# State space kernel of the first block: gains on VectorE in fewer operations, column factors and one group's masks on GpSimd, fillers on TensorE

## The chip, the cores and the metric

One core of a Trainium2 chip runs the whole program in one launch. The metric is the device time of one execution in microseconds (us). Five engines work beside each other, each through its own list of instructions in order: TensorE (PE; its weight loads are shown as PEld), VectorE (DVE), ScalarE (ACT), GpSimd (POOL) and SyncE (SP, which only issues DMAs here). They wait for each other through semaphores. The execution that was profiled has its own time and its own span (first to last instruction); the sums below are made against that one.

## The reference, cut to what matters

Eight layers follow each other on x of 2 x 512 x 128 floats: attention and feed-forward blocks of several kinds. The change touches the first layer alone. There, per batch of 512 tokens:

```
scores = q k / sqrt(32) over 77 context rows, 4 heads;  attn = softmax of the 32 largest, 0 elsewhere
c_t    = (mean of attn over the heads) @ V                       # film input
x      = layernorm(x) * (1 + gate * scale_in(c_t)) + gate * shift_in(c_t)
dt = exp(log_dt);  dtA = dt * (A_re + i A_im);  dC = (C_re + i C_im) * (exp(dtA) - 1) / A
K[d, l] = 2 * Re sum_n dC[d, n] * exp(dtA[d, n] * l)             # 128 channels, 64 states, l < 512
y = causal convolution of x with K (by DFT), + x * D_skip
y = y * (1 + gate * scale_out(c_t)) + gate * shift_out(c_t);  x_text + y, feed-forward, layernorm
```

All values are float32.

## The kernel before, in words

Tokens are 8 tiles of 128 (tile t: 4 tiles to a batch). Two strands run side by side in this layer and meet in the DFT on TensorE.

**The scores strand.** ScalarE copies the scores s0 of each tile out of PSUM. VectorE takes the tiles in four groups of two (`vec_top`, L422): four rounds of eight MAX8 (L429) and eight MATCH_REPLACE8 (L440) strike the 32 largest of each row out of r0; after the first round L437 makes nb0 (the maximum, negated). ScalarE makes exp into e0 (`act_exps0`, L455) and the sums over the 32 (`act_sums0`, L462). VectorE then zeroes what was not struck (`vec_mask0`, L443: one operation a tile, r0 < limit times e0, L447) and makes the weights w0 (`vec_weight0`, L449, L452 and L453). ScalarE writes diagonals of w0 (`act_diag`, L479), TensorE sums the heads (L509), ScalarE copies (L489), TensorE makes the film (L516), ScalarE and VectorE (`vec_film`, L745 and L748) read it; the result xk goes to the DFT.

**The state space strand.** l is split in 32 x 16, so K is a matrix product of 128 partitions (64 states, real and imaginary part) between a column factor hh4 (32 values of l a channel) and a row factor gg4 (16 values). GpSimd makes the angles and multiplies them out (`pool_s4`, L644 and L647). VectorE takes off whole turns (`vec_phase`, L558: a tensor_scalar L560 and a scalar_tensor_tensor L561 over 2176 or 2048 elements a partition, in `vec_s4` for three tensors: columns, cosines gg4, sines sG). ScalarE makes sines (`act_s4_columns`, `act_s4_turns`) and decays (eH, eG at L688). VectorE multiplies hh4 by eH in eight operations of 512 (L577). GpSimd computes the gains al and be of each state from 24 operations of 128 (`pool_s4_gains`, L600 to L623) and then, in four quarters of the channels, the row factor (`pool_s4_rows`, L658 to L661: gg4 * al + sG * be, times eG). As each quarter arrives, TensorE multiplies 32 channels (`pe_kernel`, L706, 64 records of 16 columns in the trace) and ScalarE copies (`act_kernel`, L718).

Each engine's order is written out by hand (TensorE L2708, ScalarE L2759, GpSimd L2822, VectorE L2881). On TensorE it is: three kernel quarters, film of group 0, the last quarter, film of group 1, the DFT of K (L772), the DFT of batch 0 (L758), film of group 2, and so on. SP's load of the DFT matrices waits until VectorE has read the angles that lie in the same memory (L357). GpSimd has after the rows: x2 (`pool_x2`, the normalised x times g plus b, L736 and L737), `pool_add_row` (L257, b_out onto X), the skip terms (`pool_skip`, L836 to L839). `st.link` makes the engine wait for the instruction just issued. `pe_spin` (L267) issues matmuls whose result nobody reads.

Of the kernel before, what the change touches and what calls it, by code (L numbers as in the profile page):

```python
# [83 lines left out]
def program(nc, A, out):  # L84

    ctx = ExitStack()
    with ctx:
# [240 lines left out]
        gg4, sG, eG = (part(arenaB, 8416 + 2048 * i, D, LB) for i in range(3))  # L328
        V_H, V_GC, V_GS, V_HH = 3, 4, 5, 6
        s4_vec, s4_pe, s4_inverses = sem("s4_vec"), sem("s4_pe"), sem("s4_inverses")  # L330

# [90 lines left out]
        def vec_top(dve, st, g, rounds):  # L422
            if rounds[0] == 0:
                dve.wait_ge(s0_copy, 2 * g + 2)
            for k in rounds:
                src = s0 if k == 0 else r0
                for t in GROUPS[g]:
                    for h in range(H0):
                        ins = nc.vector.max(top0[:, t, h, 8 * k:8 * k + 8], src[:, t, h, :])  # L429
                if k < KEEP // 8 - 1:  # L430
                    st.link(ins)
                else:
                    ins.then_inc(top_ready, 1)
# [7 lines left out]
                st.link(ins)  # L441

        def vec_mask0(dve, g):  # L443

            for t in GROUPS[g]:
                dve.wait_ge(e0_ready, t + 1)
                nc.vector.scalar_tensor_tensor(e0[:, t], r0[:, t], 0.5 * NEVER, e0[:, t], ALU.is_lt, ALU.mult).then_inc(em_ready, 1)  # L447
# [102 lines left out]

        A_ARE, A_ANG, A_VH, A_UG, A_GAIN = 2, 3, 4, 5, 6
        E_TANH, E_ANG, E_H, E_X2, E_COLS, E_GC, E_GS, E_ROWS = 1, 2, 3, 4, 6, 7, 8, 9
# [19 lines left out]
        def vec_s4_columns(dve):  # L572

            dve.wait_ge(s4_act, E_COLS)
            for d in range(0, D, D // 8):
                r = slice(d, d + D // 8)
                ins = nc.vector.tensor_tensor(hh4[:, r], hh4[:, r], eH[:, r], ALU.mult)  # L577
            ins.then_inc(s4_vec, 1)

        em1, half_sin, full_sin, u0, inv_a2, u1, u2, u3 = (q[i][:] for i in (0, 1, 2, 3, 4, 5, 6, 7))  # L580

        def vec_s4_inverses(dve, st):
# [9 lines left out]
            L(Vv.reciprocal(u1, u2))  # L592
            Vv.tensor_tensor(u1, u1, em1, ALU.mult).then_inc(s4_inverses, 1)

        def pool_s4_gains(pool, st):
            L = st.link
            tt, ts = nc.gpsimd.tensor_tensor, nc.gpsimd.tensor_scalar
            pool.wait_ge(s4_inverses, 1)
            pool.wait_ge(s4_act, E_ANG)
            ts(em1, u1, 2.0, None, ALU.mult)  # L600
            L(tt(u0, half_sin, half_sin, ALU.mult))
            L(ts(u0, u0, 2.0, None, ALU.mult))
            tt(u2, em1, full_sin, ALU.mult)
            L(tt(u1, em1, u0, ALU.mult))
            tt(u2, u2, full_sin, ALU.add)
            L(tt(u1, em1, u1, ALU.subtract))
            L(tt(u1, u1, u0, ALU.subtract))
            tt(u0, u1, V["are"], ALU.mult)
            L(tt(u3, u2, V["aim"], ALU.mult))
            tt(u2, u2, V["are"], ALU.mult)  # L610
            L(tt(u0, u0, u3, ALU.add))
            tt(u0, u0, inv_a2, ALU.mult)
            L(tt(u3, u1, V["aim"], ALU.mult))
            L(tt(u2, u2, u3, ALU.subtract))
            L(tt(u2, u2, inv_a2, ALU.mult))
            tt(u1, V["cre"], u0, ALU.mult)
            L(tt(u3, V["cim"], u2, ALU.mult))
            L(tt(u1, u1, u3, ALU.subtract))
            ts(al[:], u1, 2.0, V["sgn"], ALU.mult, ALU.mult)
            tt(u2, V["cre"], u2, ALU.mult)  # L620
            L(tt(u3, V["cim"], u0, ALU.mult))
            L(tt(u1, u2, u3, ALU.add))
            ts(be[:], u1, -2.0, None, ALU.mult).then_inc(s4_pool, 1)  # L623
            pool.wait_ge(s4_pool, A_GAIN)

# [26 lines left out]
        def pool_s4_rows(pool, st, slices):  # L652
            L, tt = st.link, nc.gpsimd.tensor_tensor
            pool.wait_ge(s4_act, E_ROWS)
            for i in slices:
                r = slice(i * D // 4, (i + 1) * D // 4)
                gq, sq, n = gg4[:, r, :], sG[:, r, :], D // 4
                tt(gq, gq, bc(al[:, r], P, n, LB), ALU.mult)  # L658
                L(tt(sq, sq, bc(be[:, r], P, n, LB), ALU.mult))
                L(tt(gq, gq, sq, ALU.add))  # L660
                tt(gq, gq, eG[:, r, :], ALU.mult).then_inc(s4_pool, 1)  # L661
# [29 lines left out]
        def act_s4_turns(act):  # L691
            A_ = nc.scalar.activation
            act.wait_ge(s4_vec, V_GC)
            A_(gg4[:], gg4[:], ACT.Sin, scale=-TURN, bias=V["qturn"]).then_inc(s4_act, 1)
            act.wait_ge(s4_vec, V_GS)
            A_(sG, sG, ACT.Sin, scale=-TURN, bias=V["oturn"]).then_inc(s4_act, 1)

        def pe_kernel(pe, i):

            pe.wait_ge(s4_vec, V_HH)  # L700
            pe.wait_ge(s4_pool, A_GAIN + 1 + i)
            if i >= 2:
# [2006 lines left out]
        def _(pe):  # L2709
# [50 lines left out]
        def _(act):  # L2760
# [62 lines left out]
        def _(pool):  # L2823
# [58 lines left out]
        def _(dve):  # L2882
# [63 lines left out]
def _packed(I):  # L2946
# [9 lines left out]
    def chunks(a):  # L2956
# [89 lines left out]
```

## Time and profile before

| | us |
|---|---|
| three runs | 521.46, 520.95, 516.23; median 520.95 |
| profiled execution, its time | 518.91 |
| its span | 517.1 |
| busy in the span: PE, DVE, ACT, POOL | 448.2, 363.3, 280.2, 214.3 |

In the rows below, a time of the timeline is "start, length, engine, line, operation, out<-in, count"; in brackets stands what ended the idle time before. An operation that is held up by another engine's hold on memory shows as a longer operation, not as idle time. [...]

### The profile page before, as it was taken

How to read it: one execution, taken by the hardware profiler on the slowest of the kernel's cores; microseconds unless marked ns; L12 is line 12 of the kernel's file. 1: busy time of each engine (PE TensorE's matmuls, PEld its weight loads, DVE VectorE, ACT ScalarE, POOL GpSimd, SP SyncE). 2: the span in 40 equal slices, each digit the busy share in tenths (PEclk: the TensorE clock that was granted, in tenths of full speed). 3: DMA queues.
4: the chain of work that ended last, by engine and by line, in shares of the span. 5: the costliest groups of instructions: out<-in, count | busy, mean ns of one | idle time of the engine just before them, and what ended most of it. 6: DMA issues, size and time to landing. Idle time of an engine off the chain costs nothing.

```text
span 517.1 us, 9756 instructions
## 1 busy us (share of the span) xinstructions
PE 448.2 (87%) x3171; PEld 330.7 (64%) x3171; DVE 363.3 (70%) x1329; ACT 280.2 (54%) x891; POOL 214.3 (41%) x242
## 2 busy tenths in 40 slices
PE   3970489999888999998878998999899999699986
PEld 2320489889663467677745654677569997378855
DVE  4799988956568377685379585887673245889675
ACT  2698477641422566663334553666425567779543
POOL 4999996031114540000040155312447758423341
PEclk9665559999999999999997999999999999899999
DMA  7207000000419000000000141000346981100001
GB/s 253 96 1 308 12 1 3 2 1 1 162 40 419 18 2 1 1 2 2 1 0 12 38 114 35 1 2 1 99 129 196 298 271 55 41 0 2 1 0 43
DMA packets 20536, 34.45 MB, mean 67 GB/s; under 512 B 2627, under 2 KB 14083, under 8 KB 19942
## 3 DMA queue, kind: packets, MB, share of 16 engines
q1 hardware_dynamic: 19014, 30.80, 17.8%
q0 software_dynamic: 1472, 3.03, 1.6%
q8 instruction: 26, 0.43, 0.3%
q14 instruction: 24, 0.20, 0.1%
HBM read 29.00 MB, written 6.81 MB: 69 GB/s over the span
## 4 chain that ended last, share of the span: by engine, by line
PE 60%; DVE 14%; POOL 11%; DMA 5%; ACT 4%; issue 3%; SPq 1%; ACTq 0%; DVEq 0%; POOLq 0%
PE bank L270 3%; PE bank L1055 3%; PE bank L2385 3%; PE bank L792 3%; PE bank L1101 3%; PE bank L1082 3%; PE bank L2351 3%; PE bank L1998 2%; PE bank L706 2%; PE bank L1725 2%; DVE arenaB L440 2%; PE bank L1698 2%; PE bank L2375 2%; PE bank L263 2%; PE bank L874 1%
## 5 line engine op out<-in xcount | busy, mean ns | idle before, releaser
L270 PE MATMUL bank<-in_ctx 128*128 128x512 f32 (+2 forms) x130 | 43.5, 464 | 0.0
L219 POOL TENSOR_SCALAR rtmp<-mv 128x4 f32<-128x4 f32 x12 | 3.0, 253 | 95.6 <-DVE mv L198 77.0
L2096 POOL DMA_INDIRECT ys_scratch<-arenaB,home x30 | 28.9, 964 | 10.7 <-ACT arenaB L2055 7.1
L2430 ACT ACTIVATE arenaB<-bank,arenaB 128x77 f32<-128x77 f32 x88 | 27.2, 355 | 7.4 <-DVE arenaB L2471 7.4
L270 PEld LDWEIGHTS bank<-in_ctx 128*128 128x128 f32 x130 | 21.4, 198 | 14.8 <-issue 13.9
L2240 DVE TENSOR_TENSOR in_ffn<-in_dft,bank 128x256 f32<-128x256 f32 x30 | 12.4, 420 | 25.6 <-PE bank L2016 17.7
L1112 DVE TENSOR_REDUCE nmax<-bank 128x1 f32<-128x512 f32 x32 | 20.5, 685 | 13.2 <-PE bank L1055 13.2
L440 DVE MATCH_REPLACE8 arenaB<-arenaB 128x77 f32<-128x77 f32 x128 | 26.8, 223 | 0.0
L1165 ACT ACTIVATE arenaB<-bank,nmax 128x512 f32<-128x512 f32 x32 | 21.7, 683 | 4.3 <-DVE nmax L1112 2.6
L2343 POOL TENSOR_TENSOR arenaB<-arenaB 128x385 f32<-128x385 f32 x8 | 13.4, 1679 | 19.8 <-DVE arenaB L2333 19.8
L277 ACT COPY xnT<-bank 128x512 f32<-128x512 f32 x14 | 8.4, 597 | 24.4 <-PE bank L263 24.4
L226 POOL TENSOR_SCALAR rtmp<-mv 128x4 f32<-128x4 f32 x10 | 2.5, 248 | 45.8 <-DVE mv L198 39.6
L2065 ACT ACTIVATE in_dft<-bank 128x256 f32<-128x256 f32 x30 | 11.5, 383 | 17.8 <-PE bank L1998 17.8
L2089 POOL DMA_INDIRECT xs_scratch<-arenaB,slot x16 | 15.7, 981 | 12.4 <-issue 12.4
L2430 ACT ACTIVATION_READ_ACCUMULATOR arenaB<-bank,arenaB 128x1 f32 x88 | 20.8, 237 | 0.0
L2351 PE MATMUL bank<-arenaB,xnT 128*128 128x385 f32 (+1 forms) x48 | 20.1, 556 | 0.0
L1998 PE MATMUL bank<-in_dft 128*128 128x128 f32 x144 | 19.1, 276 | 1.0 <-DMA in_dft<-in_moe_dram 1.0
L429 DVE MAX8 arenaB<-arenaB 128x8 f32<-128x77 f32 x128 | 19.5, 225 | 0.3
L2385 PEld LDWEIGHTS bank<-arenaB 128*128 128x128 f32 (+1 forms) x160 | 18.6, 192 | 1.0 <-issue 0.7
L2385 PE MATMUL bank<-arenaB 128*128 128x128 f32 (+1 forms) x160 | 19.0, 275 | 0.0
L263 PE MATMUL bank<-in_ctx,xn 128*128 128x128 f32 x56 | 13.2, 335 | 6.4 <-DVE xn L233 6.1
L233 DVE TENSOR_SCALAR xn<-X,mv,rstd 128x128 f32<-128x128 f32 x56 | 16.0, 349 | 3.7 <-POOL rstd L220 2.8
(511 smaller groups left out, 1375.7 us busy)
## 6 DMA issues: line engine op xcount, KB each, us to landing
in_dft<-in_moe_dram SPq DMA_DIRECT2D x18, 256.0 KB
arenaA<-in_moe_dram SPq DMA_DIRECT2D x1, 3840.0 KB
tmp<-in_moe_dram SPq DMA_DIRECT2D x12, 256.0 KB
in_dft<-in_dft_dram SPq DMA_DIRECT2D x1, 2048.0 KB, 7.7
in_dft<-in_head_dram SPq DMA_DIRECT2D x1, 2048.0 KB, 7.6
arenaA<-in_l_dram SPq DMA_DIRECT2D x1, 2048.0 KB
xs_scratch<-in_spare_dram SPq DMA_DIRECT2D x2, 975.0 KB
arenaB<-xs_scratch SPq DMA_DIRECT2D x6, 260.0 KB, 4.8
```

The lines of the kernel that those rows point to most:

```text
L233: nc.vector.tensor_scalar(dst[:, t, :], src[:, t, :], mv[:, t, 0:1], rstd[:, t:t + 1], ALU.subtract, ALU.mult).then_inc(ln_done, 1)
L263: ins = nc.tensor.transpose(bank[banks[t // TB]][:, (t % TB) * P:(t % TB + 1) * P], src[:, t, :], ident)
L270: nc.tensor.matmul(bank[into][:, 0:width], ident, packed["ctx"][:, 0:width], start=True, stop=True)
L429: ins = nc.vector.max(top0[:, t, h, 8 * k:8 * k + 8], src[:, t, h, :])
L440: ins = nc.vector.match_replace(r0[:, t, h, :], top0[:, t, h, 8 * k:8 * k + 8], src[:, t, h, :], NEVER)
L1112: Vv.tensor_reduce(nmax0[:, t, h:h + 1], bank[2 * (n % 2) + i][:], AX.X, ALU.max, negate=True).then_inc(sc_max, 1)
L1165: nc.scalar.activation(pb0[:, n % 2, i, :], bank[2 * (n % 2) + i][:], ACT.Exp, bias=nmax0[:, t, h:h + 1], accum_out=rsum0[:, t, h:h + 1]). ...
L1998: ins = nc.tensor.matmul(bank[i % 4][:, c * P:(c + 1) * P], wtile[i % AHEAD][:, c * P:(c + 1) * P], xsT[:, g % 2, (i - i0) * P:(i - i0 + 1 ...
L2096: nc.gpsimd.indirect_dma_start(out=A[f"ys_scratch{b}"], out_offset=bass.IndirectOffsetOnAxis(ap=home[:, b, j:j + 1], axis=0), in_=ys[b][:, ...
L2351: nc.tensor.matmul(bank3(n, i)[:, 0:(h1 - h0) * NC], xnT[:, n * P:(n + 1) * P], f3[:, n // TB, h0:h1, :].rearrange("p h k -> p (h k)"), st ...
L2385: ins = nc.tensor.matmul(bank[6 + t % 2][:, 0:P], pT3[0:w, t % 2, c, :], vw3[0:w, t // TB, c, :], start=(c == 0), stop=(c == CK3 - 1))
L2430: ins = nc.scalar.activation(p3[:, n % 3, h, :], bank3(n, i)[:, (h - h0) * NC:(h - h0 + 1) * NC], ACT.Exp, bias=mx3[:, n % 3, h:h + 1], ac ...
```

## The change

- The sine of the row factor is no longer made from phases of its own: the cosine's phase is the sine's absolute value shifted. `vec_s4` takes the first phase with offset 0, and one scalar_tensor_tensor (max of the value and its negative) replaces the second `vec_phase`. Both turns on ScalarE then wait for V_GS.
- The 24 operations of `pool_s4_gains` become 18 on VectorE (`vec_s4_gains`), which stand after `vec_s4`, in front of group 1 of the scores.
- The eight column multiplications go to GpSimd (`pool_s4_columns`), after `pool_gate`, `pool_add_row` and both `pool_x2`, which now stand ahead of the rows; the rows wait for VectorE's gains.
- The masks of group 2 go to GpSimd (`pool_mask0`, four operations of 308, after the rows); VectorE's mask of group 3 waits for them, and group 3's first round of `vec_top` is moved ahead of the weights of group 2.
- ScalarE's copies for a later layer's folded weights are split around the decays of the rows, exponentials of group 1 move ahead of the first kernel quarter.
- TensorE gets fillers of 512 columns: four after the folds, one after each of the first two kernel quarters.

```diff
-            vec_phase(st, gg4, gg4, uG, V["quarter"]).then_inc(s4_vec, 1)
-            vec_phase(st, sG, sG, uG, V["off2"]).then_inc(s4_vec, 1)
-            dve.wait_ge(s4_vec, V_GS)
+            vec_phase(st, gg4, gg4, uG, 0.0).then_inc(s4_vec, 1)
+            dve.wait_ge(s4_vec, V_GC)
+            nc.vector.scalar_tensor_tensor(sG, gg4, -1.0, gg4, ALU.mult, ALU.max).then_inc(s4_vec, 1)
...
+        def vec_s4_gains(dve, st):
+            dve.wait_ge(s4_act, E_ANG)
+            stt(u0, half_sin, 2.0, half_sin, ALU.mult, ALU.mult)
+            L(stt(u2, em1, 1.0, full_sin, ALU.add, ALU.mult))
+            tt(al[:], u2, V["aim"], ALU.mult)
+            L(stt(u3, em1, 1.0, u0, ALU.add, ALU.mult))
...
+            stt(be[:], em1, V["sgn"], half_sin, ALU.mult, ALU.add).then_inc(s4_vec, 1)
...
+        def pool_mask0(pool, st):
+            pool.wait_ge(em_ready, 4)
+            pool.wait_ge(top_final, 1)
+            for t in GROUPS[2]:
+                st.link(nc.gpsimd.tensor_scalar(r0[:, t], r0[:, t], 0.5 * NEVER, None, ALU.is_lt))
+                pool.wait_ge(e0_ready, t + 1)
+                nc.gpsimd.tensor_tensor(e0[:, t], r0[:, t], e0[:, t], ALU.mult).then_inc(em_ready, 1)
...
         def pool_s4_rows(pool, st, slices):
-            pool.wait_ge(s4_act, E_ROWS)
+            pool.wait_ge(s4_vec, V_GAIN)
+            pool.wait_ge(s4_act, E_GS)
...
 # TensorE
             pe_fold1(pe)
+            pe_spin(0, 4, S)
             pe_kernel(pe, 0)
+            pe_spin(0, 1, S)
             pe_kernel(pe, 1)
+            pe_spin(0, 1, S)
...
 # GpSimd
-            pool_s4_gains(pool, st)
             pool_gate(pool)
-            pool_s4_rows(pool, st, range(4))
+            pool_add_row(pool, V["b_out"], NT)
             pool_x2(pool, st, 0)
             pool_x2(pool, st, 1)
-            pool_add_row(pool, V["b_out"], NT)
+            pool_s4_columns(pool)
+            pool_s4_rows(pool, st, range(4))
+            pool_mask0(pool, st)
...
 # VectorE
             vec_s4(dve, st)
-            vec_s4_columns(dve)
+            vec_s4_gains(dve, st)
             vec_top(dve, st, 1, range(4))
...
-            vec_top(dve, st, 2, range(2, 3))
+            vec_top(dve, st, 2, range(2, 4))
             vec_film(dve, st, 1)
-            vec_top(dve, st, 2, range(3, 4))
-            vec_mask0(dve, 2)
+            vec_top(dve, st, 3, range(1))
             vec_weight0(dve, st, 2)
-            vec_top(dve, st, 3, range(4))
+            vec_top(dve, st, 3, range(1, 4))
             vec_mask0(dve, 3)
```

## Rows read from the trace of the kernel before

**Rows 1.** Windows by stage: second half of the first layer's DFT.
```profile
104.00:135.00 31.00, 30.78 (x241) 28.31 (x242) 15.79 (x46) 6.54 (x27) 6.33 (x6) 1.00 0.00 1
```

**Rows 2.** Chain that ended last, in order of time (start, length, engine, line).
```profile
29.44 0.50 POOL xt L600
...
54.04 1.02 POOL arenaB L658
...
63.73 3.57 PE bank L706 x64
```

**Rows 3.** Timeline of VectorE: phases, columns, start of group 1.
```profile
30.68 1.39 DVE L560 TENSOR_SCALAR arenaB<-arenaA,in_cols 128x2176 f32<-128x2176 f32 x1
32.11 2.55 DVE L561 SCALAR_TENSOR_TENSOR arenaA<-arenaB,arenaA 128x2176 f32<-128x2176 f32 x1
...
38.44 1.48 DVE L560 TENSOR_SCALAR arenaB<-in_dft,in_cols 128x2048 f32<-128x2048 f32 x1
...
42.41 6.87 DVE L577 TENSOR_TENSOR arenaA<-arenaA 128x512 f32<-128x512 f32 x8
49.20 1.21 DVE L429 MAX8 arenaB<-arenaB 128x8 f32<-128x77 f32 x8
```

**Rows 4.** Timeline of GpSimd: a gain, row angles, x2, b_out, skip.
```profile
25.21 4.24 POOL L647 TENSOR_TENSOR in_dft<-tmp,in_cols 128x512 f32<-128x512 f32 x4
...
32.34 2.63 POOL L604 TENSOR_TENSOR xt<-xt 128x128 f32<-128x128 f32 x1
...
76.33 1.27 POOL L736 TENSOR_TENSOR tmp<-tmp,in_rows 128x512 f32<-128x512 f32 x1
...
78.90 2.36 POOL L257 TENSOR_TENSOR X<-X,in_rows 128x1024 f32<-128x1024 f32 x1
...
86.93 1.26 POOL L838 TENSOR_TENSOR tmp<-tmp,xnT 128x512 f32<-128x512 f32 x1
88.27 1.39 POOL L839 TENSOR_TENSOR tmp<-tmp,xn 128x512 f32<-128x512 f32 x1
```

**Rows 5.** Timeline of VectorE: masks and small operations beside GpSimd, last mask alone.
```profile
66.03 1.20 DVE L437 TENSOR_SCALAR nb<-arenaB 128x8 f32<-128x8 f32 x1
...
74.05 1.00 DVE L453 TENSOR_TENSOR w<-w,tmask 128x8 f32<-128x8 f32 x1
...
86.99 3.01 DVE L447 SCALAR_TENSOR_TENSOR arenaB<-arenaB 128x308 f32<-128x308 f32 x2
...
102.48 0.87 DVE L447 SCALAR_TENSOR_TENSOR arenaB<-arenaB 128x308 f32<-128x308 f32 x2
```

**Rows 6.** Timeline of VectorE: operations of 128; the first is waited for.
```profile
12.58 0.28 DVE L587 TENSOR_TENSOR xt<-in_s 128x128 f32<-128x128 f32 x1
12.90 0.29 DVE L588 TENSOR_TENSOR xt<-xt 128x128 f32<-128x128 f32 x1
```

**Rows 7.** Timelines of ScalarE and TensorE: column sine, row decays, diagonals, last quarter, DFT.
```profile
37.02 2.10 ACT L683 ACTIVATE arenaA<-arenaA,in_cols 128x2048 f32<-128x2048 f32 x1
...
45.73 3.75 ACT L688 ACTIVATE arenaB<-tmp 128x128 f32<-128x128 f32 x16
...
77.79 2.45 ACT L479 ACTIVATE diag<-in_ctx,w 128x128 f32<-128x128 f32 x8
...
77.36 2.20 PE L706 MATMUL bank<-arenaB,arenaA 128*32 128x16 f32 x64
...
83.44 7.31 PE L772 MATMUL bank<-kx,in_dft 128*128 128x128 f32 x64
...
104.22 3.81 PE L758 MATMUL bank<-arenaA,in_dft 128*128 128x128 f32 x32 [0.85 <-DVE arenaA L748]
```

**Rows 8.** Page: largest group of TensorE (the filler's line), and load of DFT matrices.
```profile
L270 PE MATMUL bank<-in_ctx 128*128 128x512 f32 (+2 forms) x130 | 43.5, 464 | 0.0
...
in_dft<-in_dft_dram SPq DMA_DIRECT2D x1, 2048.0 KB, 7.7
```

**Rows 9.** Windows of two us: score matmuls at half clock.
```profile
32.00:34.00 2.00, 2.00 (x4) 0.65 (x3) 1.97 (x2) 1.98 (x8) 2.00 (x2) 0.50 0.00 0
```

More of the change, by code:

```diff
@@ L328, in program @@
         gg4, sG, eG = (part(arenaB, 8416 + 2048 * i, D, LB) for i in range(3))
-        V_H, V_GC, V_GS, V_HH = 3, 4, 5, 6
-        s4_vec, s4_pe, s4_inverses = sem("s4_vec"), sem("s4_pe"), sem("s4_inverses")
+        V_H, V_GC, V_GS, V_GAIN, V_HH = 3, 4, 5, 6, 7
+        s4_vec, s4_pe, top_final = sem("s4_vec"), sem("s4_pe"), sem("top_final")
         def quarters():
@@ L440, in vec_top @@
                         ins = nc.vector.match_replace(r0[:, t, h, :], top0[:, t, h, 8 * k:8 * k + 8], src[:, t, h, :], NEVER)
-                st.link(ins)
+                if g == 2 and k == KEEP // 8 - 1:
+                    ins.then_inc(top_final, 1)
+                else:
+                    st.link(ins)
+        def pool_mask0(pool, st):
[5 more added lines that the diff above has]
+                nc.gpsimd.tensor_tensor(e0[:, t], r0[:, t], e0[:, t], ALU.mult).then_inc(em_ready, 1)
         def vec_mask0(dve, g):
+            if g == 3:
+                dve.wait_ge(em_ready, 6)
             for t in GROUPS[g]:
@@ L549, in pe_dt @@
             nc.tensor.matmul(bank[7][:, 0:D], V["avg"], dtd, start=True, stop=True).then_inc(s4_pe, 1)
-        A_ARE, A_ANG, A_VH, A_UG, A_GAIN = 2, 3, 4, 5, 6
+        A_ARE, A_ANG, A_VH, A_UG, A_HH = 2, 3, 4, 5, 6
         E_TANH, E_ANG, E_H, E_X2, E_COLS, E_GC, E_GS, E_ROWS = 1, 2, 3, 4, 6, 7, 8, 9
@@ L567, in vec_s4, with pool_s4_columns @@
             dve.wait_ge(s4_vec, V_H)
-            vec_phase(st, gg4, gg4, uG, V["quarter"]).then_inc(s4_vec, 1)
-            vec_phase(st, sG, sG, uG, V["off2"]).then_inc(s4_vec, 1)
-            dve.wait_ge(s4_vec, V_GS)
-        def vec_s4_columns(dve):
-            dve.wait_ge(s4_act, E_COLS)
+            vec_phase(st, gg4, gg4, uG, 0.0).then_inc(s4_vec, 1)
+            dve.wait_ge(s4_vec, V_GC)
+            nc.vector.scalar_tensor_tensor(sG, gg4, -1.0, gg4, ALU.mult, ALU.max).then_inc(s4_vec, 1)
+        def pool_s4_columns(pool):
+            pool.wait_ge(s4_act, E_COLS)
             for d in range(0, D, D // 8):
                 r = slice(d, d + D // 8)
-                ins = nc.vector.tensor_tensor(hh4[:, r], hh4[:, r], eH[:, r], ALU.mult)
-            ins.then_inc(s4_vec, 1)
+                ins = nc.gpsimd.tensor_tensor(hh4[:, r], hh4[:, r], eH[:, r], ALU.mult)
+            ins.then_inc(s4_pool, 1)
         em1, half_sin, full_sin, u0, inv_a2, u1, u2, u3 = (q[i][:] for i in (0, 1, 2, 3, 4, 5, 6, 7))
@@ L592, in vec_s4_inverses @@
             L(Vv.reciprocal(u1, u2))
-            Vv.tensor_tensor(u1, u1, em1, ALU.mult).then_inc(s4_inverses, 1)
-        def pool_s4_gains(pool, st):
+            Vv.scalar_tensor_tensor(em1, u1, 2.0, em1, ALU.mult, ALU.mult)
+        def vec_s4_gains(dve, st):
             L = st.link
[L597 to L607, printed above, removed]
+            tt, stt = nc.vector.tensor_tensor, nc.vector.scalar_tensor_tensor
+            dve.wait_ge(s4_act, E_ANG)
[3 more added lines that the diff above has]
+            L(stt(u3, em1, 1.0, u0, ALU.add, ALU.mult))
+            tt(be[:], u2, V["are"], ALU.mult)
+            L(tt(u1, em1, u3, ALU.subtract))
@@ L608, in pool_s4_gains @@
             tt(u0, u1, V["are"], ALU.mult)
[L609 to L612, printed above, removed]
             L(tt(u3, u1, V["aim"], ALU.mult))
-            L(tt(u2, u2, u3, ALU.subtract))
-            L(tt(u2, u2, inv_a2, ALU.mult))
+            tt(u0, u0, al[:], ALU.add)
+            L(tt(u2, be[:], u3, ALU.subtract))
+            stt(u0, u0, 2.0, inv_a2, ALU.mult, ALU.mult)
@@ L616, in pool_s4_gains @@
+            L(stt(u2, u2, 2.0, inv_a2, ALU.mult, ALU.mult))
             tt(u1, V["cre"], u0, ALU.mult)
[L617 to L624, printed above, removed]
+            tt(u3, V["cim"], u2, ALU.mult)
@@ L628, in pool_s4 @@
+            tt(em1, V["cre"], u2, ALU.mult)
+            L(tt(half_sin, V["cim"], u0, ALU.mult))
+            stt(al[:], u1, V["sgn"], u3, ALU.mult, ALU.subtract)
+            stt(be[:], em1, V["sgn"], half_sin, ALU.mult, ALU.add).then_inc(s4_vec, 1)
         def pool_s4(pool, st):
@@ L657, in pool_s4_rows @@
                 gq, sq, n = gg4[:, r, :], sG[:, r, :], D // 4
-                tt(gq, gq, bc(al[:, r], P, n, LB), ALU.mult)
-                L(tt(sq, sq, bc(be[:, r], P, n, LB), ALU.mult))
-                L(tt(gq, gq, sq, ALU.add))
+                tt(gq, gq, bc(be[:, r], P, n, LB), ALU.mult)
+                L(tt(sq, sq, bc(al[:, r], P, n, LB), ALU.mult))
+                L(tt(gq, sq, gq, ALU.subtract))
+                if i == slices[0]:
+                    pool.wait_ge(s4_act, E_ROWS)
                 tt(gq, gq, eG[:, r, :], ALU.mult).then_inc(s4_pool, 1)
@@ L692, in act_s4_turns @@
             A_ = nc.scalar.activation
-            act.wait_ge(s4_vec, V_GC)
-            A_(gg4[:], gg4[:], ACT.Sin, scale=-TURN, bias=V["qturn"]).then_inc(s4_act, 1)
             act.wait_ge(s4_vec, V_GS)
+            A_(gg4[:], gg4[:], ACT.Sin, scale=-TURN).then_inc(s4_act, 1)
             A_(sG, sG, ACT.Sin, scale=-TURN, bias=V["oturn"]).then_inc(s4_act, 1)
         def pe_kernel(pe, i):
-            pe.wait_ge(s4_vec, V_HH)
-            pe.wait_ge(s4_pool, A_GAIN + 1 + i)
+            pe.wait_ge(s4_pool, A_HH + 1 + i)
             if i >= 2:
@@ L1215, in act_fold1, with act_fold1_out @@
             nc.scalar.copy(bm1[:], bank[3][0:DC, 0:D]).then_inc(fold1_copy, 1)
+        def act_fold1_out(act):
             act.wait_ge(fold1_mm, 3)
@@ L2773, in _ @@
             act_s4_turns(act)
+            act_fold1(act)
             act_s4_rows(act)
+            act_fold1_out(act)
             act_exps0(act, 0)
@@ L2777, in _ @@
             act_vfilm(act)
-            act_fold1(act)
+            act_exps0(act, 1)
             act_kernel(act, 0)
-            act_exps0(act, 1)
+            act_sums0(act, 1)
             act_kernel(act, 1)
-            act_sums0(act, 1)
             act_diag(act, 0)
@@ L2978, in _packed @@
         "alt": np.tile([1.0, -1.0], (P, 1)), "quarter": np.repeat([0.25, 0.0], P // 2)[:, None],
-        "off2": np.repeat([0.0, 0.25], P // 2)[:, None], "qturn": TURN * np.repeat([0.25, 0.0], P // 2)[:, None], "oturn": TURN * np.repeat([0.0, 0.25], P // 2)[:, None],
+        "off2": np.repeat([0.0, 0.25], P // 2)[:, None], "qturn": TURN * np.repeat([0.25, 0.0], P // 2)[:, None], "oturn": np.full((P, 1), 0.25 * TURN),
         "sgn": np.repeat([1.0, -1.0], P // 2)[:, None],
```

2 lines of the change are left out of this document (1 added, 1 removed).

## The prediction

> **What bounds the kernel now.** I read the windows first, then the chain of waits, then each engine's timeline where the chain changes engine. In the windows TensorE is busy for 30.78 of the 31 us from 104 to 135 [rows 1]: whatever is worth having in this layer lies ahead of that. The chain of waits names the owner: GpSimd from 29.44 (the gains) through 54.04 (the first row operation) to TensorE's second kernel quarter at 63.73 [rows 2]; and at 104.22 begins the DFT's second batch, for which TensorE waited 0.85 us on VectorE [rows 7]. From that instant TensorE decides, so a delay of it at about 83 or 104 reaches the end of the span in full, and an early arrival is worth as much as VectorE is early too.
>
> The timelines tell why 24 operations of 128 on GpSimd took 24 us. One of them lasted 2.63 us from 32.34 on [rows 4]; that is VectorE's scalar_tensor_tensor of 2.55 us from 32.11 on [rows 3]. It goes the other way as well: two masks on VectorE took 3.01 us beside GpSimd's skip operations of 1.26 and 1.39 us and 0.87 us alone, and an operation on eight numbers took 1.20 us [rows 4, 5]. Laid on one time line, VectorE's first mask (86.99) begins to work when L838 ends (88.2), L839 then waits for it, and the second mask ends (90.0) after L839 (89.66). So the two engines take turns, one whole instruction each, whenever both read this memory with two inputs or VectorE runs a tensor_scalar; MAX8 and MATCH_REPLACE8 are not held. The eight columns bear it out: 6.87 us, 0.86 each, one small GpSimd operation to each of them [rows 3].
>
> **The change, part by part.** I take four holds from these rows: a GpSimd operation of 512 holds 1.1 us (1.06 back to back at L647, 1.27 whole at L736 [rows 4]); a VectorE tensor_scalar of 2048 or 2176 holds 1.2 (1.39 less the end of a small GpSimd operation), a scalar_tensor_tensor of that size 2.3 (2.55 likewise), an operation of 128 holds 0.2 of its 0.28 [rows 3, 6].
>
> *Phases.* One tensor_scalar (1.48 [rows 3]) goes. Five long operations stay, with other company. GpSimd is free at 29.44, does the gate (256 wide, under the 1.27 us of an operation of 512, and VectorE is in MATCH_REPLACE8) and begins to add b_out by 30.4 to 30.7, with VectorE's phase due at 30.68; were the phase first, the order of the turns changes and their sum does not. That addition is 2.36 us long [rows 4], so the phase starts at 32.8. From there they take turns: VectorE 34.0, x2 35.1, VectorE 37.4, x2 38.5, VectorE 39.7, x2 40.8, VectorE 43.0, x2 44.1, absolute value 46.4. Before, this stretch ended at 42.41 [rows 3]. So 1.5 us saved and 5.5 lost: +4.0.
>
> *Columns and gains.* The columns' sines are ready by then (they need only the first phase, at 37.4, and two sines of ScalarE of 2.1 us [rows 7]), so GpSimd's eight operations of 512 meet VectorE's 18 gains. Eight turns of 1.1 + 0.2 take 10.4 us: 56.8. Ten gains are left, alone: 0.28 each, 2.8 us (0.32 where the next waits for it [rows 6]). VectorE is through at 59.6, and GpSimd's rows, which wait for it, begin at 59.6 where they began at 54.04: +5.6. By the row, eight columns take 6.87 us on VectorE and at least 8.5 on GpSimd; I cost them by their own rows, 1.1 each.
> [...]
>
> *ScalarE.* Both turns now follow the absolute value; then the folds' copies and the row decays (3.75 us [rows 7]). They end near 56, needed only at the last operation of the first quarter, after 62. Nothing. If the gains were 6 us earlier than I say, they would bind.
>
> *Scores on VectorE.* Group 1 starts at 59.6 instead of 49.20 [rows 3]: +10.4. From there to the weights of group 1 (74.05 + 1.00 [rows 5]) was 25.85 us, of which some 5 were turns given to GpSimd's rows. The rows last four quarters of 4.85 (54.04 to 63.73 is two) and end at 79.0, so the second pair of masks and weights is no longer held: 1.8 us less. Weights of group 1: 59.6 + 24.05 = 83.65. ScalarE began the diagonals from them at 77.79 [rows 7], then idle capacity of 2.7 us; now it begins at 83.65, +5.9. From the diagonals to the DFT of K there were 5.65 us (77.79 to 83.44 [rows 7]), and the last kernel quarter (rows at 79.0, matmuls after film 0) is done by 83. The DFT starts at 89.3.
>
> *Masks of group 2.* 3.01 us leave VectorE [rows 5]. Four GpSimd operations of 308, each under the 2.36 us of one of 1024, start when the last round of group 2 is struck (about 91) and end before 100; the film of group 2 needs them at 105, VectorE's mask 3 at 105. Behind them waits only the skip of batch 0, needed at the first result, after 120. Nothing, with 5 us of cover.
>
> *End of the layer.* VectorE's chain, three us lighter and delayed by 8.6 at 83.65, reaches film 2 at 105; TensorE reaches it 5.9 late. So of the 0.85 us that TensorE waited at 104.22 some 0.5 go. Sum: +5.9 - 0.5 = **+5.4 us**.
>
> *Fillers and DMA.* Six fillers of 0.46 us at mostly full clock [rows 8] lie in TensorE's waits for the rows: a quarter of 3.57 us plus one filler, 4.0 to 4.5, fits the 4.85 between quarters. The DFT load goes out 4 us later (46.4), takes 7.7 [rows 8] and is needed at 89. Both nothing.
>
> The profiled execution took 518.91 us (517.1 of span). 518.91 + 5.4 = **524.3 us**. The median shown is 2.0 above the profiled time, so by it the same step would read 526.4.
>
> **Bounds.** Twelve GpSimd operations of 512 at 1.06 instead of 1.1 give 0.5 back, at 1.27 cost 2.0 more; turns that VectorE wins now and then give up to 2 back. Alone, my case is 522 to 527.
>
> **Rivals.**
>
> *A, forecast: the two engines take turns and the rows start late.* 524.3. Chance 0.45.
>
> *B, half of it: the long phases are held, but VectorE's short gains slip through beside the columns.* For it: no row shows two-input operations of 128 on VectorE against operations of 512 on GpSimd for long. Then the gains end near 51, the columns at 55, rows +1.0, group 1 +1.8, both inside the slack of 2.7 us. If the fillers also bring TensorE to the full clock one quarter earlier, a quarter costs 2.20 instead of 3.57 us [rows 2, 7]. Together +1 to -2: 517 to 520. Chance 0.18.
>
> *C, other side: faster.* Mechanism: GpSimd's operations don't delay VectorE here, only their own completion. Place: 30.7 to 46. The phases end at 41, the gains at 45.5, group 1 starts 3.7 us earlier; with the masks gone VectorE reaches film 2 about 6.7 earlier. GpSimd: 32.8, x2 37.9, columns from 41 to 48, rows 6 us earlier. Price -6.3: 512.6. It decides as soon as rows start before 54.04 and group 1 before 49.20. Against it stand three rows [rows 5]. Chance 0.22.
>
> *D: A, and TensorE meets the DFT at half clock.* In A TensorE waits between the films, from 75 to 89, where it ran through before. The DFT of K at half clock would take up to twice 7.31 us [rows 7]; half of that at half clock is +3.7: 528. The rows are of two minds: at 32 to 34 TensorE was busy all the time and the granted clock was 0.50 [rows 9].
> [...] Chance 0.15.
>
> **How the numbers follow.** What a measurement of this kernel can tell from no change is about 1%, 5.2 us. A lies just at it: half of its chance is within. Faster: C but for a little, 0.21. Within 1%: B and half of A, 0.41. Slower: half of A and D, 0.38. A and D hold 0.6, B and C 0.4, so the range has to take in C: 512 to 530; the likeliest case's own is 522 to 527.
>
> **What would show it.** In the changed kernel: VectorE's first phase longer than 3 us, since it begins under the b_out addition (C: 1.4); the column operations on GpSimd spaced by 1.3 us with a gain between each two (B and C: 1.06); the first row operation at 59 to 60 (C: 48); group 1's first MAX8 at 59 to 60 (C: 45); the DFT of K starting at 89 (C: 77); the granted clock at that start (D: 0.50). If the rows begin before 54, or the b_out addition doesn't push the phase, the prediction is wrong.

## The result, and the profile after

| | before | after |
|---|---|---|
| median of four runs each, us | 520.44 | 525.29 |
| profiled execution, us | 518.91 | 524.83 |
| its span, us | 517.1 | 523.0 |

The ratio of the medians is 1.0105, with a 95% interval of 1.0066 to 1.0145: the change makes the kernel slower by about 1%, 4.85 us by the medians. 524.3 us had been forecast, 5.4 us above the profiled execution of the kernel before.

VectorE's timeline of the changed kernel (start, length, engine, line, operation, operands, count) answers to [rows 3] and [rows 6]:

```profile
31.26 3.14 DVE L573 TENSOR_SCALAR arenaB<-arenaA,in_cols 128x2176 f32<-128x2176 f32 x1
...
43.31 3.23 DVE L583 SCALAR_TENSOR_TENSOR arenaB<-arenaB 128x2048 f32<-128x2048 f32 x1
46.47 1.36 DVE L612 SCALAR_TENSOR_TENSOR xt<-xt 128x128 f32<-128x128 f32 x1
...
55.41 1.35 DVE L619 TENSOR_TENSOR xt<-xt,in_s 128x128 f32<-128x128 f32 x1
56.80 0.29 DVE L620 TENSOR_TENSOR xt<-xt,tmp 128x128 f32<-128x128 f32 x1
...
59.06 0.35 DVE L629 SCALAR_TENSOR_TENSOR tmp<-xt,in_cols 128x128 f32<-128x128 f32 x1
59.32 1.21 DVE L429 MAX8 arenaB<-arenaB 128x8 f32<-128x77 f32 x8
...
83.40 0.17 DVE L466 TENSOR_TENSOR w<-w,tmask 128x8 f32<-128x8 f32 x1
```

And GpSimd's, which answers to [rows 4]:

```profile
30.90 2.35 POOL L257 TENSOR_TENSOR X<-X,in_rows 128x1024 f32<-128x1024 f32 x1
...
35.59 3.33 POOL L741 TENSOR_TENSOR tmp<-tmp,in_rows 128x512 f32<-128x512 f32 x1
...
44.37 12.25 POOL L590 TENSOR_TENSOR arenaA<-arenaA 128x512 f32<-128x512 f32 x8
59.48 1.06 POOL L662 TENSOR_TENSOR arenaB<-arenaB,tmp 128x512 f32<-128x512 f32 x1 [2.87 <-DVE tmp L629]
...
77.69 1.26 POOL L667 TENSOR_TENSOR arenaB<-arenaB 128x512 f32<-128x512 f32 x1
90.62 0.99 POOL L450 TENSOR_SCALAR arenaB<-arenaB 128x308 f32<-128x308 f32 x1 [11.67 <-DVE arenaB L440]
```

Read the two side by side. The first phase, 1.39 us before, takes 3.14 beside the b_out addition; GpSimd's x2 products, of which one took 1.27 us before [rows 4], take up to 3.33 beside VectorE's long operations, and its eight column products 12.25 beside the last phase and the gains. Eight gains take 1.24 to 1.36 us each while GpSimd does its eight columns, and the ninth, L620 at 56.80, takes 0.29 again. The rows wait 2.87 us for the last gain.

TensorE's timeline answers to [rows 7]:

```profile
64.30 2.20 PE L710 MATMUL bank<-arenaB,arenaA 128*32 128x16 f32 x64 [2.35 <-POOL arenaB L667]
...
74.06 3.60 PE L710 MATMUL bank<-arenaB,arenaA 128*32 128x16 f32 x64 [0.55 <-POOL arenaB L667]
77.58 3.58 PE L522 MATMUL bank<-diag,arenaB 128*77 128x128 f32 x16
...
82.83 2.20 PE L710 MATMUL bank<-arenaB,arenaA 128*32 128x16 f32 x64
84.98 2.24 PE L522 MATMUL bank<-diag,arenaB 128*77 128x128 f32 x16
...
89.26 7.31 PE L776 MATMUL bank<-kx,in_dft 128*128 128x128 f32 x64
...
109.55 3.81 PE L762 MATMUL bank<-arenaA,in_dft 128*128 128x128 f32 x32 [0.36 <-DVE arenaA L752]
```

The DFT of K begins at 89.26 (83.44 before), the second batch's products at 109.55 (104.22): +5.33 of the span's +5.9. From 74.06 to the end of L522 at 87.2 TensorE has no idle time, and in the middle it runs at half the clock. The windows (from:to, length, PE busy and count, granted TensorE clock as a share of full speed, DMA share, GB/s; in [rows 1] and [rows 9] the busy times and counts of PE, PEld, DVE, ACT and POOL stand between length and clock) show where:

```profile
68.00:70.00 2.00, 0.98 (x31) 1.00 0.00 0
70.00:72.00 2.00, 2.00 (x40) 0.67 0.00 0
...
80.00:82.00 2.00, 2.00 (x12) 0.77 0.00 0
82.00:84.00 2.00, 2.00 (x42) 1.00 0.00 0
```

The start of the first phase differs from profile to profile (30.68 us in the kernel before, 30.85 to 32.52 in the twelve others, among which no edit stands ahead of it). So kernels are compared below by instants counted from that start ("from the phase").

| from the phase, us | rows start | third quarter starts | group 1's weights done | DFT of K | second batch |
|---|---|---|---|---|---|
| before | 23.33 | 37.96 | 44.37 | 52.76 | 73.54 |
| changed | 28.22 | 42.80 | 52.31 | 58.00 | 78.29 |

From the second batch's products to the end of the span the thirteen profiles, these two and the eleven of the runs, have 411.0 to 413.7 us left, in no order that goes with an edit; those differences I leave unexplained.

### The profile page after: what moved, and what is told of

Same layout as the page of the kernel before. It is cut to its first block, busy times and chain, and to the rows that moved or that the text cites. A ratio compares the mean times of both kernels' runs of the same rounds, so it can differ in the third digit from the quotient of the medians.

```text
span 523.0 us, 9775 instructions
## 1 busy us (share of the span) xinstructions
PE 453.5 (87%) x3183; PEld 330.6 (63%) x3183; DVE 368.8 (71%) x1336; ACT 279.8 (53%) x891; POOL 213.2 (41%) x230
## 4 chain that ended last, share of the span: by engine, by line
PE 63%; DVE 18%; POOL 5%; DMA 5%; ACT 4%; issue 3%; SPq 1%; ACTq 0%; DVEq 0%; POOLq 0%
PE bank L270 3%; PE bank L1059 3%; PE bank L2390 3%; PE bank L796 3%; PE bank L1105 3%; PE bank L762 3%; PE bank L1086 3%; PE bank L2356 2%; PE bank L2003 2%; PE bank L1730 2%; PE bank L1703 2%; PE bank L263 2%; PE bank L2380 2%; PE bank L878 1%; PE bank L522 1%
## 5 line engine op out<-in xcount | busy, mean ns | idle before, releaser
L270 PE MATMUL bank<-in_ctx 128*128 128x512 f32 (+2 forms) x142 | 52.1, 498 | 3.6 <-ACT vw L1224 3.6
L270 PEld LDWEIGHTS bank<-in_ctx 128*128 128x128 f32 x142 | 24.2, 203 | 21.5 <-issue 16.5
L2021 PE MATMUL bank<-arenaA,in_ffn 128*128 x120 | 18.5, 277 | 1.0 <-DVE in_ffn L2245 1.0
```

What stands on the lines that cost most here:

```text
L270: nc.tensor.matmul(bank[into][:, 0:width], ident, packed["ctx"][:, 0:width], start=True, stop=True)
L2021: ins = nc.tensor.matmul(bank[4 + t % 2][:, 0:P], hids[:, t % 3, c * P:(c + 1) * P], V["moe"][:, 2 * HE + c * P:NE * WE][:, bass.ds(off[t] ...
```

## The experiments

The theory (T1): GpSimd's wide products and VectorE's two-operand operations hold each other up, one whole instruction at a time; the work set ahead of the rows delays phases, gains, rows and group 1 alike. In the profile after, gains of 0.29 us alone take 1.24 to 1.36 beside the column products. There are three groups of runs, each with its own runs of the kernel before (medians 519.61, 519.92 and 519.82); a ratio is taken to those of its group, with its 95% interval in brackets.

**Additions and x2 back behind the rows.**

```diff
-            pool_add_row(pool, V["b_out"], NT)
-            pool_x2(pool, st, 0)
-            pool_x2(pool, st, 1)
             pool_s4_columns(pool)
             pool_s4_rows(pool, st, range(4))
+            pool_x2(pool, st, 0)
+            pool_x2(pool, st, 1)
+            pool_add_row(pool, V["b_out"], NT)
```

> GpSimd's addition of b_out and its two x2 products are put back behind the rows; all else as in the changed kernel. Theory T1 (GpSimd's wide operations and VectorE's two-operand operations hold each other up instruction by instruction, so that work set ahead of the rows delays phases, gains and rows alike): phases and the magnitude end at 40.5 to 41.5 us instead of 46.5; column products from about 40 still take turns with the gains and end at 50 to 52; rows and group 1's first MAX8 start at 51 to 54; DFT of K at 83 to 84.5; time 518.5 to 520.5. Rival R1 (only GpSimd's own serial work ahead of the rows counts, 13 us of it taken out): rows start at 46 to 48, DFT of K at 80 or earlier, time 515 to 517. Rival R2 (the gains' place on VectorE is what costs, the additions are hidden): time within 1 us of the changed kernel, 524 to 526.

Measured: 523.23 us, ratio 1.0058 (1.0031 to 1.0084). The first phase took 1.35 us, the phases ended at 40.9, the gains at 53.8, the rows began at 53.88: all as T1 had it (R1 had the rows at 46 to 48). But the DFT of K came at 87.59, not at 83 to 84.5. The weights of group 1 on VectorE's timeline:

```profile
79.13 2.08 DVE L466 TENSOR_TENSOR w<-w,tmask 128x8 f32<-128x8 f32 x1
```

What GpSimd did at that time:

```profile
78.61 2.57 POOL L257 TENSOR_TENSOR X<-X,in_rows 128x1024 f32<-128x1024 f32 x1
```

And TensorE's second film, which needs those weights:

```profile
82.61 3.41 PE L522 MATMUL bank<-diag,arenaB 128*77 128x128 f32 x16 [3.15 <-issue]
```

With the rows early, the weights of group 1 alone decide: they are done at 81.21, 50.07 from the phase. The addition, moved back, now holds their last product (eight numbers a partition) for 2.08 us, against 0.17 in the changed kernel. ScalarE begins the diagonals made from them at 81.24; TensorE waits 3.15 us and then runs at half the clock. So of the 4.8 to 6.3 us that T1 expected at the DFT of K 1.7 came (89.26 to 87.59): the second strand gave back most of it, and the time missed T1's 518.5 to 520.5.

**Columns after the gains** (the additions stay ahead).

```diff
+            pool.wait_ge(s4_vec, V_GAIN)
             pool.wait_ge(s4_act, E_COLS)
             for d in range(0, D, D // 8):
```

> GpSimd's eight column products wait until VectorE has finished the gains; the additions stay ahead of them. Nothing is left out or added but that wait. T1: the gains run undisturbed in 4.5 to 5.5 us (18 operations of 0.28 and one or two turns) and end near 51.3; group 1 starts there, 8 us earlier than in the changed kernel; columns 51.3 to 60, rows start at 60, as late as in the changed kernel. So the weights of group 1 stop deciding and the rows alone do: DFT of K at 88 to 89, time 523 to 525. Rival R2 (what counts is VectorE's scores, late by 10 us): the DFT of K follows them, 81 to 83, time 517 to 519.

Measured: 527.35 us, ratio 1.0139 (1.0103 to 1.0175). The gains after the first took 0.28 to 0.35 us, group 1's weights were done at 46.07 from the phase (52.31 in the changed kernel), and it helped nothing: rows at 60.76, DFT of K at 91.24, 60.39 from the phase. R2 falls, and T1's sizes were too small by 2.2 us or more (88 to 89 for the DFT, 523 to 525 for the time). The columns alone took 9.89 us, so the rows began 1.7 us later than in the changed kernel (29.91 from the phase, 28.22 there). TensorE's rows show the rest:

```profile
65.71 3.52 PE L711 MATMUL bank<-arenaB,arenaA 128*32 128x16 f32 x64 [5.16 <-POOL arenaB L668]
69.17 2.08 PE L270 MATMUL bank<-in_ctx 128*128 128x512 f32 x2
71.17 3.60 PE L711 MATMUL bank<-arenaB,arenaA 128*32 128x16 f32 x64
```

At half the clock a quarter and one filler are 5.6 us, more than the 4.8 of a row quarter, and TensorE's queue no longer has a gap: the filler pushes the third quarter, whose rows were done at 75.65, to 76.71.

**No fillers.** The six filler products of the change are left out.

```diff
-            pe_spin(0, 4, S)
             pe_kernel(pe, 0)
-            pe_spin(0, 1, S)
             pe_kernel(pe, 1)
-            pe_spin(0, 1, S)
             pe_kernel(pe, 2)
```

> The six filler products between the kernel's quarters are left out; nothing else. T1: quarters 1 and 2 run at half the clock (3.6 us instead of 2.2 to 2.5) beside GpSimd's rows of 4.85 us each, which hides it; the third quarter and the first FiLM products were at half clock already; the DFT of K starts within 0.3 us of 89.3; time 524.5 to 525.8. Rival R3a (the fillers take TensorE's time and cost): 523 to 524, DFT of K at 88 or earlier. Rival R3b (without them the clock is still half at the DFT of K, 64 products at twice the time): that stage 14.6 instead of 7.3 us, time 528 to 532.

Measured: 523.99 us, ratio 1.0074 (1.0047 to 1.0100). The first three quarters took 3.57 to 3.60 us, and the DFT of K began 58.45 from the phase, at full clock, so R3b falls. The time is R3a's and half a microsecond under T1's, but R3a's earlier DFT did not come (58.00 in the changed kernel). The fillers neither helped nor hurt by an amount that these runs can tell.

**Both: additions behind the rows, columns after the gains.**

> Both edits of the first two runs: additions and x2 behind the rows, and the column products wait for the gains. T1: phases end at 41, gains at 44 to 45 undisturbed, group 1 starts there (49.2 in the kernel before); columns 44 to 53 on GpSimd beside the scores, rows start at 52 to 53 (54.0 before), last row quarter at 72 to 73, DFT of K at 81 to 82.5; time 516.5 to 519.5, that is 0.995 to 1.00 of the kernel before. Rival R2b (VectorE's scores decide the DFT of K, and are now 5 us earlier than before): DFT of K at 78 to 80, time 514 to 516. Rival R5 (the loss is not ahead of the DFT of K at all): time stays at 524 to 525.

Measured: 522.23 us, ratio 1.0041 (1.0016 to 1.0066). The phases ended as T1 had them, and all gains took 0.28 to 0.35 us (the last was done 14.4 from the phase), with group 1's weights done at 40.47. But eight columns of 9.87 us together lie between gains and rows, and the rows begin at 24.33, 2.5 us or more later than T1 had them. From the third quarter (39.79) TensorE worked for 15.1 us with 0.15 us idle, half of it at the lower clock (granted clock 0.50 in the windows up to 79 us, which is 46.7 from the phase): DFT of K at 54.89. R2b falls, since the weights are 3.9 us earlier than in the kernel before and the DFT of K is 2.1 later; so does R5, since 3.1 us came at the DFT of K. That is better than either edit alone, but not the forecast 516.5 to 519.5.

**Columns by quarter.** On top of both, GpSimd does two columns before each row quarter instead of eight before the first.

```diff
             for i in slices:
+                pool_s4_columns(pool, i)
...
-            pe.wait_ge(s4_pool, A_HH + 1 + i)
+            pe.wait_ge(s4_pool, A_HH + i)
```

> On top of both edits (additions and x2 behind the rows, columns after the gains), GpSimd computes the two column products that a quarter of the kernel needs just before that quarter's rows, instead of all eight first; the same operations. Fillers as in the changed kernel. T1b (the third quarter's rows set when TensorE's third quarter starts, and from there 14.5 to 15.2 us of TensorE at half the clock lead to the DFT of K, as in all kernels so far but the first run): counted from the first phase's start, the third quarter's rows are done 2.4 us earlier, the DFT of K starts 52 to 53 us after the phase's start (before 52.8, changed 58.0, both edits alone 54.9), time 517.5 to 520. Rival T1c (TensorE, at half the clock with fillers between, is itself the queue from the first quarter on): 53 to 54.5, time 519 to 521.

Measured: 517.82 us, ratio 0.9966 (0.9941 to 0.9991). The third quarter starts at 36.50 instead of 39.79, 3.3 us earlier where 2.4 had been expected, and the DFT of K at 51.80 (T1b had 52 to 53, T1c 53 to 54.5). The third quarter still met the lower clock (3.60 us, after 4.16 us without work).

**More fillers in that version**: `pe_spin(0, 2, S)` and `pe_spin(0, 4, S)` after the first two quarters.

> As the run before, with 2 fillers after the first quarter and 4 after the second instead of one each. If that keeps the granted clock at full to the third quarter, third quarter and first FiLM products take 2.2, 2.2 and 1.9 us (3.6, 3.6 and 1.9 to 2.1 at half the clock): DFT of K 50 to 51.5 us after the first phase's start, time 516 to 518.5. If the clock falls all the same, each further filler takes 2.08 us on TensorE's queue (5 more: up to 10 us, less what lay idle): DFT of K at 54 to 58 after the first phase, time 521 to 525.

Measured: 516.48 us, ratio 0.9929 (0.9904 to 0.9953), DFT of K at 51.33. (There are four more fillers, one and three, not the five of the expectation.) TensorE's rows of this run:

```profile
68.98 2.20 PE L711 MATMUL bank<-arenaB,arenaA 128*32 128x16 f32 x64 [0.18 <-POOL arenaB L668]
71.11 1.97 PE L522 MATMUL bank<-diag,arenaB 128*77 128x128 f32 x16
...
76.63 2.71 PE L711 MATMUL bank<-arenaB,arenaA 128*32 128x16 f32 x64 [1.82 <-POOL arenaB L668]
79.27 2.97 PE L522 MATMUL bank<-diag,arenaB 128*77 128x128 f32 x16
```

The clock held through third quarter and first film; then came 1.82 us without work, and the next two groups took 2.71 and 2.97 us, where 2.20 and 1.97 are the full clock's.

**Columns that only write.**

```diff
-                ins = nc.gpsimd.tensor_tensor(hh4[:, r], hh4[:, r], eH[:, r], ALU.mult)
+                ins = nc.gpsimd.memset(hh4[:, r], 0.01)
```

> The changed kernel with GpSimd's eight column products replaced by eight constant fills of the same extents: the column decays are left out (the output differs), GpSimd still writes the same bytes but reads no operands. T1 (operands of the two engines are what they take turns over): the gains run at 0.28 us each from 46.5 and end at 51 to 52.5, rows start there, 7 to 8 us earlier than in the changed kernel, DFT of K near 83 to 84, time 518 to 520. Rival (any GpSimd work of that width, writes alone too, holds VectorE): gains still 1 us or more apart while the fills run, end later than 53.

Measured: 516.52 us, ratio 0.9951 (0.9921 to 0.9982), below T1's 518 to 520. GpSimd's fills:

```profile
46.87 3.78 POOL L590 MEMSET arenaA<- 128x512 f32 x8
```

VectorE's gains, which begin before them and end after them:

```profile
45.73 1.35 DVE L612 SCALAR_TENSOR_TENSOR xt<-xt 128x128 f32<-128x128 f32 x1
47.00 0.28 DVE L613 SCALAR_TENSOR_TENSOR xt<-xt 128x128 f32<-128x128 f32 x1
...
51.16 0.34 DVE L629 SCALAR_TENSOR_TENSOR tmp<-xt,in_cols 128x128 f32<-128x128 f32 x1
```

Beside the fills the gains take 0.28 to 0.35 us (1.24 to 1.36 beside the products in the changed kernel); the first one is still held, by the x2 product before them. The rows begin 20.04 from the phase (28.22 in the changed kernel) and the DFT of K at 50.72. So what VectorE's gains wait for in the changed kernel is GpSimd's reading of operands, not GpSimd's being busy or its writes. The gains are the place to read that: the whole time also holds that eight fills take 3.78 us where the products took 12.25.

TensorE is early in this run, waits before the second film, and does it at half the clock:

```profile
77.09 3.61 PE L522 MATMUL bank<-diag,arenaB 128*77 128x128 f32 x16 [0.99 <-issue]
```

**The changed kernel again.**

> The changed kernel unaltered, beside the others on the same chip. All theories: 4 to 6 us above the kernel before, 1.008 to 1.012. It gives the changed kernel's median on this chip, against which the runs without fillers and with the additions back are read.

Measured: 524.85 us, ratio 1.0100 (1.0063 to 1.0137). In this profile the clock was at half already in the first quarter:

```profile
65.59 3.59 PE L710 MATMUL bank<-arenaB,arenaA 128*32 128x16 f32 x64 [2.16 <-POOL arenaB L667]
69.11 2.08 PE L270 MATMUL bank<-in_ctx 128*128 128x512 f32 x2
71.12 3.60 PE L710 MATMUL bank<-arenaB,arenaA 128*32 128x16 f32 x64
```

The third quarter starts 44.13 from the phase; without fillers, also at half the clock, it was 42.82. So fillers at half the clock can cost 1.3 us at the third quarter. Little of it reaches the DFT of K: 58.53 here, 58.00 in the first profile, 58.45 without fillers.

**The gap filled too**: `pe_spin(0, 2, S)` between the first film and the fourth quarter of the version with more fillers.

> The version with columns by quarter and fillers 4, 2, 4, and 2 more fillers between the first FiLM products and the fourth quarter, where TensorE lay idle for 1.8 us and the clock then fell. If the clock holds: fourth quarter 2.2 us and second FiLM products 2.0 (2.7 and 3.0 in that run), DFT of K 50 to 50.7 us after the first phase's start (51.3 in that run), time 515 to 516.5, 0.989 to 0.994 of the kernel before. If the idle stretch was not what let the clock fall: no change, 516 to 517.

Measured: 515.38 us, ratio 0.9932 (0.9895 to 0.9969). Its TensorE rows from the filler on:

```profile
74.23 1.88 PE L270 MATMUL bank<-in_ctx 128*128 128x512 f32 x4
76.22 2.20 PE L711 MATMUL bank<-arenaB,arenaA 128*32 128x16 f32 x64
78.34 1.97 PE L522 MATMUL bank<-diag,arenaB 128*77 128x128 f32 x16
```

The clock held to the DFT of K (granted clock 1.00 in all windows of 2 us from 56 to 92 us), which starts at 49.82, 1.5 us earlier than without these two fillers; the second batch starts at 70.11 (73.54 before). Both versions beat the kernel before by 0.7%; the times don't tell them apart.

**Masks of group 2 back on VectorE** (the changed kernel otherwise).

```diff
-            vec_top(dve, st, 2, range(2, 4))
+            vec_top(dve, st, 2, range(2, 3))
             vec_film(dve, st, 1)
-            vec_top(dve, st, 3, range(1))
+            vec_top(dve, st, 2, range(3, 4))
+            vec_mask0(dve, 2)
             vec_weight0(dve, st, 2)
-            vec_top(dve, st, 3, range(1, 4))
+            vec_top(dve, st, 3, range(4))
...
-            pool_mask0(pool, st)
```

> The changed kernel with group 2's masks back on VectorE and VectorE's order there as in the kernel before. By the prediction's step (masks on GpSimd take half a microsecond off TensorE's idle time before the second batch's products, and nothing else): DFT of K unchanged at 58 to 58.5 us after the first phase's start, idle ahead of the second batch's products 0.85 us or a little more instead of 0.36, that is 0.5 us later; time 524.5 to 526.5. Rival: the masks on GpSimd hold VectorE up, then without them it is 1 us or more faster, 522 to 524.

Measured: 526.54 us, ratio 1.0123 (1.0091 to 1.0154). DFT of K 58.84 from the phase, and TensorE's wait ahead of the second batch is the 0.85 us of before again:

```profile
111.60 3.81 PE L757 MATMUL bank<-arenaA,in_dft 128*128 128x128 f32 x32 [0.85 <-DVE arenaA L747]
```

So the masks, with VectorE's order around them, are worth the 0.49 us that the prediction gave them; the rival falls. The DFT of K is 0.3 us later than expected, in a profile where TensorE was at half the clock from the second quarter on (3.60 us), so the rest of the time is not to be put to the masks.

**More fillers in the changed kernel** (6, 2 and 3).

> The changed kernel with 6, 2 and 3 fillers instead of 4, 1 and 1. If the clock then holds through the third quarter and the first FiLM products (2.2 and 2.0 us instead of 3.6 and 3.6), the rows' path is 2.5 us shorter, but the weights of group 1 still come at 52.3 us after the first phase's start, so that the DFT of K starts 57 to 58 us after it (58.0 and 58.5 in the changed kernel's two profiles): a gain of 0 to 1 us, time 523.5 to 525.5. Rival (the rows and the clock alone decide the stage): DFT of K at 55.5 to 56, time 521.5 to 523.

Measured: 524.96 us, ratio 1.0093 (1.0060 to 1.0127), a time in T1's range; but the DFT of K began 60.20 from the phase, which neither theory had, 1.7 to 2.2 us later than in the changed kernel's two profiles. TensorE's timeline:

```profile
74.83 2.20 PE L710 MATMUL bank<-arenaB,arenaA 128*32 128x16 f32 x64
77.51 2.24 PE L522 MATMUL bank<-diag,arenaB 128*77 128x128 f32 x16 [0.48 <-ACT diag L492]
...
81.84 2.20 PE L710 MATMUL bank<-arenaB,arenaA 128*32 128x16 f32 x64
85.75 3.67 PE L522 MATMUL bank<-diag,arenaB 128*77 128x128 f32 x16 [1.72 <-issue]
89.22 3.16 PE L529 MATMUL bank<-vfilm,amT 128*128 128x256 f32 x8
```

And the windows of the same stretch, columns as above:

```profile
80.00:84.00 4.00, 4.00 (x72) 1.00 0.01 4
84.00:86.00 2.00, 0.28 (x3) 0.74 0.02 4
86.00:88.00 2.00, 2.00 (x11) 0.50 0.00 0
```

ScalarE makes the diagonals of group 1 at that time:

```profile
84.38 2.44 ACT L492 ACTIVATE diag<-in_ctx,w 128x128 f32<-128x128 f32 x8 [2.00 <-DVE w L466]
```

The clock did hold through the third quarter and the first film (2.20 and 2.24 us). TensorE was done early and waited 1.72 us; the profile names no releaser, but the wait ends 1.4 us into these diagonals, which the second film reads. In that wait the granted clock fell from 1.00 to 0.50, and the second film took 3.67 and 3.16 us instead of 2.24 and 1.99. A path shortened ahead of a wait that does not move gave nothing.

Not tried: the new phases and gains alone in the kernel before, and ScalarE's new order by itself; what each is worth stays open.

## Why the prediction was right, point by point

**The turns, right.** The phases ended at 46.54 (forecast 46.4), the eighth gain at 56.76 (56.8), the last at 59.41 (59.6); rows at 59.48 and group 1 at 59.32 (both 59.6). The run with write-only columns shows the cause. The eight turns had been priced at 10.4 us by the rows; the eight gains began 46.47 to 55.41 and were done after 10.3 us, so that price holds here. The prediction's "6.87 us on VectorE" against "at least 8.5 on GpSimd" is no comparison of the two engines, though: the 0.86 us on VectorE hold a turn of GpSimd's each, and an addition of 512 with both operands in this memory took VectorE 0.69 us where GpSimd computed nothing (L2232 of the kernel before, at 423 us), against GpSimd's 1.06 to 1.27. The sum went by the 1.1 and is not touched. What the prediction has as not held shows in the kernel before: eight MAX8 took 1.22 us beside GpSimd's rows (from 58.40) and 1.21 with GpSimd idle (from 90.23), a MATCH_REPLACE8 0.22 to 0.23 in both places; the tensor_scalar over eight numbers, which it has as held, took 1.20 us at 66.03 and 0.17 at 91.47 with GpSimd idle.

**From group 1 to the DFT, right in number, half right in owner.** Weights done at 83.57 (83.65), diagonals begun at 83.61 (83.65), DFT at 89.26 (89.3). But the step named the weights as what decides and had the rows' strand "done by 83". The last quarter began at 82.83 and was done at 85.0. TensorE had no gap from 74.06 to 87.2: the rows' strand, with third quarter and first film at half the clock, came out at the same instant as the weights. The runs show two owners. No run moves one strand alone, but with the rows 5.5 us earlier and the weights 2.2, the DFT of K comes 1.6 us earlier (58.00 to 56.45) and waits for the weights; with the weights 6.2 earlier and the rows 1.7 later it comes 2.4 later; with the rows 3.9 and the weights 11.8 earlier, 3.1 earlier (54.89); with both 8.2 earlier (columns that only write), 7.3 earlier.

**Some of the agreement is luck.** The absolute instants fit because this profile's first phase began 0.58 us later than before's. From the phase, the stage cost 5.24 us at the DFT of K and 4.75 at the second batch, where 5.9 and 5.4 were forecast: the terms were 0.65 us too large, the phases' sum (15.28 against 15.72) the most of it. The later start and 0.57 us behind the second batch, neither of which the prediction has, made up for it.

**Fillers, the step that was mis-sized.** "Six fillers of 0.46 us" took one record of the page for one filler. The group of that line on the page after (count, busy time, mean ns):

```profile
L270 PE MATMUL bank<-in_ctx 128*128 128x512 f32 (+2 forms) x142 | 52.1, 498 | 3.6 <-ACT vw L1224 3.6
```

That is twelve records more than in [rows 8] for six fillers, so a filler is two; it took 0.92 to 1.12 us at the full clock and 2.08 at half. "Fits the 4.85 between quarters" then fails at half the clock (3.60 + 2.08). The price of nothing held all the same: the DFT of K began at 58.00 and 58.53 from the phase with fillers and at 58.45 without.

**Masks of group 2, right.** GpSimd began them at 90.62 and was done at 94.4; TensorE's wait went from 0.85 to 0.36 us, and back to 0.85 with the masks back.

**The other steps priced at nothing, right.** The load of the DFT matrices went out at 46.58 (46.4) and took 7.6 us; ScalarE's row decays ended at 55.7 (56).

**The rivals.** B falls: gains did not slip through. C falls: GpSimd delayed VectorE everywhere it was said to. D did not happen in the changed kernel (granted clock 1.00 when the DFT began), but half the clock behind a wait between the films is what the run with more fillers showed, one stage earlier (granted clock 0.50 from 86 to 90 us, behind 1.72 us without work).

## What to carry to other kernels

Before work is moved to GpSimd to relieve VectorE, look at what VectorE does at that moment: here its operations with two operands took turns with GpSimd's products, one for one, and a short one lasted as long as the wide one that it waited for (gains of 0.29 us took 1.24 to 1.36 beside columns of 1.3 each). VectorE's tensor_scalar operations were held here as well (the first phase, 3.14 us for 1.39). Where two strands meet, trace both: a gain on one is worth only the lead that the other has. And hand the consumer its data in the pieces it waits for: two columns per quarter instead of eight ahead of all took 3.3 us off the third quarter's start, with no work removed.

## What the runs showed of the hardware

- A product over eight numbers a partition took 2.08 us beside GpSimd's addition of 1024 wide, and 0.17 alone.
- GpSimd's fills of 512 (3.78 us for eight) ran beside VectorE's two-operand operations with no delay to those (0.28 to 0.35 us each, as with GpSimd idle in the changed kernel).
- The granted clock fell from 1.00 to 0.50 in or behind waits of 1.72 and 1.82 us in two runs, and did not behind one of 1.58 us in the version with the gap filled (third quarter, 2.20 us). The length of the last wait alone does not decide it: in the run with columns that only write the clock fell behind 0.99 us without work (second film, 3.61 us), and in the changed kernel the first quarter ran at the full clock (2.20 us) behind a wait of 2.35. What makes the difference these rows don't settle. In the run with columns after the gains, TensorE was busy without a gap from 66 us on and the clock read 0.50 up to 82.
